# A two-layer attention and expert kernel: the query product's slot and the place of the experts' loads

## The reference

```
xn = layernorm(x);  x = x + attention0(xn) + ffn0(xn)
xn = layernorm(x);  x = x + attention1(xn) + experts(xn)

attention0: q,k,v = xn @ qkv_w.T + qkv_b, 16 heads of 8 features,
            softmax(q k^T / sqrt(8)) v, then @ proj_w.T + proj_b
ffn0:       (silu(xn @ wg.T) * (xn @ wu.T)) @ wd.T, weights int32 / 127, 384 hidden
attention1: heads cut from (tokens, features) by a plain reshape, so a head is a stretch of
            32 tokens; a mask of 64x64 blocks (band, first and last block, 3 drawn pairs)
experts:    softmax over 8 logits, top 2, at most 1.25*T/8 = 320 tokens by rank; each expert
            (silu(x @ g.T) * (x @ u.T)) @ d.T with 256 hidden, weighted and summed
```

## Time and profile before

| | us |
|---|---|
| three timed runs | 540.23, 537.68, 538.36 (median 538.36) |
| the profiled execution: whole time, and span | 544.03, 542.0 |
| PE busy | 454.8 (84%) |
| DVE busy | 400.5 (74%) |
| ACT busy | 328.8 (61%) |
| POOL busy | 262.5 (48%) |
| chain that ended last: PE, DVE, "issue", ACT, DMA, SP's queue | 53%, 18%, 10%, 10%, 4%, 4% |

### The profile page before, as it was taken

One profiled execution on the slowest core, in us unless ns is written; L12 is line 12 of the kernel. 1 busy time (PEld: TensorE's weight loads), 2 busy tenths in 40 slices (PEclk: granted clock), 3 DMA queues, 4 the chain that ended last, 5 costly groups with the idle time before them and its releaser, 6 DMA issues.

```text
span 542.0 us, 9302 instructions
## 1 busy us (share of the span) xinstructions
PE 454.8 (84%) x3394; PEld 169.4 (31%) x3394; DVE 400.5 (74%) x538; ACT 328.8 (61%) x422; POOL 262.5 (48%) x499
## 2 busy tenths in 40 slices
PE   3456979889988999899989898987899999999952
PEld 1101213224322433242312431221245453455511
DVE  5699778886998699869887798789876777623204
ACT  2102666776677667656676577777766567667560
POOL 6861263724425562886378657884201233163240
PEclk9755889999999999999999999999999999999995
DMA  3896596244511360626252645174731111010018
GB/s 82 238 230 89 89 343 106 93 163 146 90 43 61 118 62 4 66 72 127 25 52 39 157 43 56 41 160 68 109 52 32 45 50 50 4 44 25 21 47 219
DMA packets 143742, 48.27 MB, mean 89 GB/s; under 512 B 109890, under 2 KB 139090, under 8 KB 142866
## 3 DMA queue, kind: packets, MB, share of 16 engines
q1 hardware_dynamic: 141394, 42.93, 38.1%
q0 software_dynamic: 2304, 4.76, 2.6%
HBM read 22.81 MB, written 23.14 MB: 85 GB/s over the span
## 4 chain that ended last, share of the span: by engine, by line
PE 53%; DVE 18%; issue 10%; ACT 10%; DMA 4%; SPq 4%; POOL 1%; POOLq 0%; ACTq 0%; DVEq 0%
PE ps L763 14%; DVE mx L1114 11%; PE ps L747 9%; PE ps L732 7%; ACT PT L962 6%; PE ps L802 3%; PE ps L810 3%; PE ps L785 2%; PE ps L803 2%; SPq L433 2%; PE ps L693 2%; PE ps L825 2%; PE ps L822 2%; PE ps L786 1%; DVE th L1135 1%
## 5 line engine op out<-in xcount | busy, mean ns | idle before, releaser
L1114 DVE TENSOR_REDUCE mx<-ps 128x2 f32<-128x1024 f32 x256 | 309.4, 1223 | 73.1 <-PE ps L732 65.1
L962 ACT ACTIVATE PT<-ps 128x1024 f32<-128x1024 f32 x256 | 258.6, 1026 | 125.9 <-PE ps L747 116.5
L763 PE MATMUL ps<-PT,Vp 128*32 128x512 f32 x1024 | 138.1, 611 | 5.4 <-ACT PT L962 4.4
L732 PE MATMUL ps<-KO,QO 48*128 48x512 bf16 (+1 forms) x512 | 104.5, 406 | 39.7 <-ACT PT L962 22.6
L747 PE MATMUL ps<-QO,KO 59*128 59x512 bf16 x512 | 100.2, 390 | 3.8 <-DMA QO<-mT 2.5
L520 POOL DMA_INDIRECT y_tokens<-expert_io,meta x40 | 38.6, 964 | 71.5 <-ACT expert_io L994 48.5
L747 PEld LDWEIGHTS ps<-QO,KO 59*128 59x128 bf16 x512 | 24.6, 93 | 142.8 <-issue 87.9
L1135 DVE SCALAR_TENSOR_TENSOR th<-th,ps 128x320 f32<-128x320 f32 (+1 forms) x44 | 23.8, 541 | 35.2 <-ACT th L978 29.4
L732 PEld LDWEIGHTS ps<-KO,QO 48*128 48x128 bf16 (+1 forms) x512 | 25.6, 96 | 70.9 <-ACT PT L962 38.6
L545 POOL CAST mp<-mx 128x32 bf16<-128x32 f32 x16 | 3.4, 214 | 82.9 <-DVE mx L1114 78.7
L509 POOL DMA_INDIRECT x_places<-xe,place_i x32 | 31.9, 995 | 22.3 <-ACT PT L962 15.2
(11 more groups left out here) (166 smaller groups left out, 475.1 us busy)
## 6 DMA issues: line engine op xcount, KB each, us to landing
z<-part SPq DMA_DIRECT2D x16, 384.0 KB
z<-part SPq DMA_DIRECT2D x16, 256.0 KB
QO<-z SPq DMA_DIRECT2D x64, 48.0 KB
KO<-z SPq DMA_DIRECT2D x64, 48.0 KB
x_places<-expert_io SPq DMA_DIRECT2D x2, 1300.0 KB, 7.4
expert_io<-x_places SPq DMA_DIRECT2D x8, 320.0 KB, 3.5
QO<-z SPq DMA_DIRECT2D x6, 384.0 KB
KO<-z SPq DMA_DIRECT2D x6, 384.0 KB
```

The lines of the kernel that those rows point to most:

```text
L732: mm = pe.matmul(ps[:, 2 * pair + half, :], rows_of(QO[u % 3], half, 2 * s + jj, rows, (qt, qt + 1)), rows_of(KO[u % 3], half, 2 * s + jj, ...
L763: last = pe.matmul(ps[32 * g:32 * g + 32, PV_BANK, :], Vp[u % 2][:, k, head(s, g), :], PT[:, (2 * t + g % 2) % 4, g // 2, :], start=(s % 2 ...
L962: act.activation(PT[:, e % 4], ps[:, 2 * pair:2 * pair + 2, :], ACT.Exp).then_inc(exp_done, 1)
L1114: dve.tensor_reduce(mx[:, a, qt, col:col + 5:4], ps[:, 2 * pair:2 * pair + 2, :], AX_X, ALU.max, negate=True).then_inc(max_read, 1)
```

## The change

Two independent edits.

The query product `qk_mm(p, 0, SIDE)` moves, in units 1 to 5, from slot 2 to slot 0, and its copy on ACT from slot 3 to slot 1. The wait for that copy moves with it: `out_transposes(w, 1)` in slot 1 now wait for it, and `normalized_transposes` in slot 3 no longer do. Unit 0 keeps slots 2 and 3.

The loads of eg, eu and ed leave the start. SP issues eg and eu in unit 0 and ed in unit 1, each time between `operand_writes(p, 1)` and the operand reads, with a semaphore of their own that the experts' products wait for.

```diff
@@ sync_unit
             if p < U:
                 operand_writes(sp, p, 0)
                 operand_writes(sp, p, 1)
+                if u < 2:
+                    for dst, src in expert_loads[0:2] if u == 0 else expert_loads[2:3]:
+                        sp.dma_start(dst, src).then_inc(experts_loaded, 16)
                 if layer(p) == 0:
                     operand_reads_0(sp, p)
@@ gate_up_1
-            pe.wait_ge(loaded, N_LOAD)
+            pe.wait_ge(experts_loaded, N_EXPERT)
@@ side_mms
+            if slot == 0 and 1 <= u and p < U:
+                pe.wait_ge(mT_ready, 2 * u + 1)
+                qk_mm(pe, p, 0, SIDE)
             if slot == 1:
                 pe.wait_ge(mT_ready, 2 * u + 1)
                 if u >= 1:
+                    if p < U:
+                        pe.wait_ge(qk_f_ready, 2 * p + 1)
                     out_transposes(pe, w, 1)
                 else:
                     xnT_mms(pe, 2, SIDE)
-            if slot == 2 and p < U:
-                if u >= 1:
-                    pe.wait_ge(on_ready, 2 * w + 2)
+            if slot == 2 and u == 0:
                 qk_mm(pe, p, 0, SIDE)
             if slot == 3 and u >= 1:
-                if p < U:
-                    pe.wait_ge(qk_f_ready, 2 * p + 1)
                 normalized_transposes(pe, w)
@@ scalar_unit
-                if slot == 3 and p < U:
+                if slot == (3 if u == 0 else 1) and p < U:
                     qk_copy(act, p, 0, SIDE)
@@ loads
-                 (w_router[:], router_T), (eg[:], eg_T), (eu[:], eu_T),
-                 (ed[:], ed_T.rearrange("e (b p) d -> p e b d", p=P))]
-        N_LOAD, N_FIRST = 16 * len(loads), 16 * len(first_loads)
+                 (w_router[:], router_T)]
+        expert_loads = [(eg[:], eg_T), (eu[:], eu_T), (ed[:], ed_T.rearrange("e (b p) d -> p e b d", p=P))]
+        N_LOAD, N_EXPERT, N_FIRST = 16 * len(loads), 16 * len(expert_loads), 16 * len(first_loads)
```

More of the change, by code:

```diff
@@ L169, in build @@
         loaded = sem("loaded")
+        experts_loaded = sem("experts_loaded")
         x_loaded = [sem(f"x_loaded{b}") for b in range(B)]
```

## The result

| | time, us (median) | lowest to highest | runs |
|---|---|---|---|
| before | 539.00 | 536.99 to 541.32 | 20 |
| changed | 536.34 | 533.80 to 538.43 | 20 |

The ratio is 0.995, interval 0.9937 to 0.9963: 2.0 to 3.4 us faster, 2.7 in the middle. The forecast was 6.6 us less, 531.8 us, with a range of 529.3 to 535.0. The sign was right; the size was not, and the time lies 1.3 us outside the range. The changed kernel's profiled execution took 536.92 us (span 534.5), a typical one of its runs.

A forecast was written before the change was run, and what follows sets the result against it. The prediction took PE, over half of the chain of waits, to bound the kernel. Loads 3.2 us plus query product 3.4 us gave 6.6 us off 538.36, so 531.8 us, range 529.3 to 535.0.

The forecast's parts named there:

- The loads, 3.2 us: Unit 0, slot 8: PE's wait for mT rows goes, 2.69 us, and the slow clock with it; new place costs nothing.
- Rival (d): Unit 0, slot 8: clock did not fall in earlier timed runs, so 2.7 instead of 3.2; 532.3 us, chance 0.10.
- The query product, 3.4 us: Slots 1 to 4 of units 1 to 5 shorten by 1.0, 1.0, 0.1, 0.65 and 0.65 us.
- No new wait in slot 1: Units 1 to 5, slot 1: transposes wait only 0 to 0.1 us for the query copy.
- the cut-off: Units 3 to 5, slot 4: SP's operand transfers do not move, limiting gains to 0.1, 0.65 and 0.65 us.
- (a): Slot 1's new wait replaces the old one, some 0.3 us a unit instead of 1.0; 534.0 us, chance 0.11.
- (b): Unit 0, slot 8: mT rows still late because other transfers fill the queue; 535.0 us, chance 0.07.
- (c): Units 3 to 5: operand transfers come sooner too, so all five units gain 1.0 us; 530.2 us, chance 0.06.
- (e): Starts of units 1 and 2: moved loads bring the mT wait back, slower, some 541 us, chance 0.04.
- upper bound of that sum, 5.5: Query product's move over units 1 to 5: summed gain bounded between -1 and 5.5 us.
- Sum: Whole kernel: 3.2 + 3.4 = 6.6 us off the 538.36 us median of the runs, giving 531.8 us.
- Rival (f): Downstream, POOL's routing work at first: something with its own clock takes all the gain back; 537.5 us, chance 0.04.

The follow-up runs named there:

- the wait dropped: Kernel before, without the query product's wait for xnT in units 1 to 5, which an earlier wait covers: 545.79 us, ratio 1.0024.
- the changed kernel's fourth run: Changed kernel, unedited, timed again on the second chip beside the third experiments: 541.18 us, ratio 0.9944 to the kernel before.
- both edits: Changed kernel with unit 4's first operand reads held behind the value products and mask-row transfers issued ahead of operand reads: 536.33 us, ratio 0.9861.
- the changed kernel's third run: Changed kernel, unedited, timed again on the second chip beside the second experiments: 539.38 us, ratio 0.9921 to the kernel before.
- the wait kept: Changed kernel, but PE still waits in slot 3 of units 1 to 5 for the query copy, long made: 538.59 us, ratio 0.9893.
- the reads held back: Changed kernel, but in unit 4 SP holds first operand reads of slots 5 and later until that slot's value products are issued: 538.23 us, ratio 0.9903.
- mask rows first: Changed kernel, but both mask-row transfers are issued ahead of the operand reads instead of behind each half: 536.89 us, ratio 0.9869.

## Why the prediction was wrong, point by point

**The loads, 3.2 us: right.** 3.23 us in the traces of the first chip, 3.2 timed alone. The stop went entirely, the new place cost nothing, the queue was empty by 94 us. Rival (d) holds in part: with the query product alone and with the wait dropped, PE stops for the mT rows (1.94 and 1.85 us) and the clock does not fall. Here is the first:

```profile
77.21 0.39 PE L748 MATMUL ps<-QO,KO 59*128 59x512 bf16 x2 [1.94 <-DMA QO<-mT]
...
77.75 1.06 PE L764 MATMUL ps<-PT,Vp 128*32 128x512 f32 x8
```

Its stretch takes 29.19 us, so the loads would be worth 29.19 - 27.95 = 1.24 us in such an execution. In the other two traces with the stop (2.55 and 2.64 us) the clock fell. By the Trainium skill, "TensorE: Matmul & The Clock Gate", section "Part 1: The HAM clock gate (the "warmup" mystery)", the point of change varies from run to run. It says so of the clock's rise; for the fall the traces agree: in unit 4's value products a stop of 1.46 us led to one (the changed kernel's fourth run) and a stop of 1.47 us did not (both edits).

One reading beside this term was wrong: the operand reads do not come in pieces of 1 KB. Between 84 and 88 us of the first trace 80 of the 109 packets are 8 KB. No term of the sum used it.

**The query product, 3.4 us: right** on the first chip (3.41, unit by unit 0.89, 0.89, 0.05, 0.73, 0.85, against 1.0, 1.0, 0.1, 0.65, 0.65). On the second, units 4 and 5 gain only about 0.2 each where PE waits for ACT in slot 4: the changed kernel's third run takes 24.50 us at unit 4's start, against 24.74 in the first trace of the kernel before, which has a wait for ACT there as well. Without it unit 5's start takes 23.41 us in the fourth run. So the size of this term depends on a wait that comes and goes; I had carried unit 1's rows over to units 4 and 5 without looking at their own slot 4, where that trace had this wait.

**No new wait in slot 1, and the cut-off: right.** Rivals (a), (b), (c) and (e) did not happen. (The upper bound of that sum, 5.5, does not follow from its terms: 1.3 us a unit gives 4.0 with the cut-off and 6.5 without it.)

**The step that failed is "Sum".** It adds two terms and takes it that nothing is given back. The edit also took five instructions out of PE's stream; I had read the moved waits as conditions and not as instructions, so "what it removes" was incomplete. The cost is 2.34 us in unit 4 and 0.43 in unit 6 in the traces of the first chip; timed by the wait kept on the second it is 2.6 us against the run beside it and 1.5 against the one before. Rival (f) had the kind of loss, something downstream that takes the gain back, but at POOL's routing work, which moved along without a wait, and at a chance of 0.04; its time should have been 538.4, the median, and not 537.5.

By the Trainium skill, "Runtime: NRT & Kernel Launch", section "Instruction fetch mechanics", code comes in blocks of 16 KiB, 256 instructions, fetched while the block before is executed, and crossing a boundary is mostly hidden. The size agrees with the 27 packets of 0.44 MB and with the 7 x 256 instructions between the two stops. The hiding fails here: 2.26 us are not hidden where 256 instructions are issued within 1.7 us.

**What is left of the difference.** 6.6 less 2.3 to 2.8 leaves 3.8 to 4.3 us, and the changed kernel measured 4.2 and 4.3 on two occasions, but 2.7 at first and 3.0 the last time (each by its ratio). Part of the spread can be seen: the stop is between 1.33 and 2.26 us long, and the cut-off's wait in unit 3 draws a slow clock in one of four traces, worth 2 us. That these two make up all of it is argued, not shown. The absolute forecast was also off by 0.6 us, since the three runs of the kernel before had a median of 538.36 and twenty have 539.00.

## What to carry to other kernels

Where an engine issues some 250 tiny instructions in a burst, its own code can be a transfer with a deadline, as here: look up the instruction fetches in the queue table, and see whether one falls into the burst. A wait moved onto an instruction that already has a semaphore instruction removed one from the stream here, and the blocks behind it shifted; comparing the instruction counts at the head of the two pages shows it at once. When two edits that touch different stages bring less together than apart, look for a stop of kind "issue" that neither has alone, and keep the old count with an idle wait before blaming the edits.

## What the runs showed of the hardware that I had not expected

- PE stands still for its own code, 1.0 to 2.3 us at a time in eight traces, and goes on 1.3 to 1.6 us after the 16 KB packet has landed. Empty data queues do not prevent it (one packet between 298.81 and 299.64).
- The stop can end in a slow clock: the eight value products behind it took 1.88 us in the changed kernel's trace and 1.94 in that of the kernel before with a wait dropped, but 1.06 after the stop of 1.01 with the reads held back.
- Chips differ. The kernel before takes 539.4 us on one and 543.7 on another, and part of it may be PE's wait for ACT in slot 4 (1.2 us in the changed kernel), which no trace of the first chip has; of the kernel before itself no trace is known to be from the second. A sum of terms from a trace of one chip is not exact on another.
- Still open: why ACT and DVE idle there though PE has issued their products; whether mask rows first has to do with its absence; why four instructions delay the fetch by more than the 0.43 us that they take; and why in five of the eight traces of the second chip unit 5's value projection comes in several pieces with stops near 0.45 us, and its stretch takes 25.8 to 26.0 us in place of 24.7.
